# Selective scan with four state numbers by 32 channels on the partitions, and folds of four units every second step

## What is computed

```
xc, r  = split(x @ W_in);  xs = conv4(xc) + conv_b;  u = silu(xs)
dbc    = u @ W_x                                  # 128 columns, then B (16), then C (16)
delta  = softplus(dbc[..., :128] @ W_dt + b_dt)
h[l]   = exp(-delta[l] * A[d, n]) * h[l-1] + delta[l] * u[l] * B[l, n]     # for every d, n
y[l,d] = sum over n of h[l, d, n] * C[l, n]  + u * D
x1     = layernorm(x + (y * silu(r)) @ W_out + xs)
sel    = the 64 rows of x1 with the highest x1 @ w_router, in each batch
out    = x1 with those rows replaced by gate * (attention + MLP)(sel) + (1 - gate) * sel
result = layernorm(x1 + out)
```

## Time and profile before

| | us |
|---|---|
| median of 3 runs | 518.41 |
| lowest and highest | 515.31, 520.69 |
| the profiled execution | 517.08 |
| its span, first to last instruction | 515.3 |

### The profile page before, as it was taken

How to read it: one execution, slowest core, us unless ns; L and a number is a source line. 1 busy time by engine, 2 the same in 40 slices (tenths; PEclk the granted TensorE clock), 3 DMA queues, 4 the chain that set the end, 5 groups by cost and what they waited for, 6 DMA issues and landing times.

```text
span 515.3 us, 6513 instructions
## 1 busy us (share of the span) xinstructions
PE 430.3 (83%) x2021; PEld 256.1 (50%) x2021; DVE 299.1 (58%) x600; ACT 335.4 (65%) x736; POOL 254.3 (49%) x230
## 2 busy tenths in 40 slices
PE   5988988878889869889978689887886888999992
PEld 3433443344435434444534345444484576887881
DVE  0302473368473458856557997869569267553465
ACT  4245697795777696568699649795186298543242
POOL 2010064369456759657467956885554144332012
PEclk9999998989999979999988788979698799999997
DMA  6102400005200001401000413780210000000003
GB/s 223 41 0 83 125 32 31 20 0 128 80 22 26 16 21 31 116 20 37 25 21 2 110 55 103 227 303 23 107 58 1 2 0 1 0 3 1 1 34 129
DMA packets 18710, 29.11 MB, mean 56 GB/s; under 512 B 2698, under 2 KB 10676, under 8 KB 18420
## 3 DMA queue, kind: packets, MB, share of 16 engines
q1 hardware_dynamic: 18676, 28.70, 18.0%
HBM read 22.27 MB, written 2.23 MB: 48 GB/s over the span
## 4 chain that ended last, share of the span: by engine, by line
PE 47%; ACT 23%; DVE 8%; issue 7%; POOL 2%; ACTq 0%; POOLq 0%; DVEq 0%
ACT loop_buf L1022 10%; PE bank L535 9%; PE bank L670 7%; PE bank L551 7%; ACT front_a L1032 5%; PE bank L616 3%; PE bank L846 3%; PE bank L822 3%; PE bank L573 2%; ACT state L1056 2%; DVE state L1184 2%; PE bank L638 1%; PE bank L620 1%; PE bank L854 1%; PE bank L582 1%
## 5 line engine op out<-in xcount | busy, mean ns | idle before, releaser
L1184 DVE TENSOR_TENSOR_SCAN state<-front_a,bank 128x512 f32<-128x512 f32 x88 | 103.9, 1209 | 63.0 <-PE bank L535 37.9
L535 PE MATMUL bank<-ident,loop_buf 128*128 128x128 f32 x512 | 92.7, 302 | 37.4 <-ACT loop_buf L1022 36.9
L535 PEld LDWEIGHTS bank<-ident,loop_buf 128*128 128x128 f32 x512 | 64.4, 151 | 111.3 <-ACT loop_buf L1022 45.8
L1022 ACT ACTIVATE loop_buf<-copy,b_rows 128x256 f32<-128x256 f32 x252 | 105.2, 495 | 0.1
L1032 ACT ACTIVATE front_a<-loop_buf,a_neg 128x512 f32<-128x512 f32 x128 | 84.5, 711 | 6.3 <-DVE state L1184 3.3
L1560 POOL TENSOR_TENSOR state<-state,front_a 128x1024 f32<-128x1024 f32 x22 | 53.7, 2450 | 31.2 <-DVE state L1184 31.0
L1560 POOL TENSOR_TENSOR state<-state,c_own 128x1024 f32<-128x1024 f32 x22 | 51.8, 2358 | 31.0 <-DVE state L1184 31.0
L1184 DVE TENSOR_TENSOR_SCAN copy<-front_a,bank 128x512 f32<-128x512 f32 x40 | 47.6, 1212 | 33.2 <-PE bank L535 20.4
L551 PE MATMUL bank<-front_c,conv_raw 128*128 128x512 f32 x128 | 60.9, 608 | 2.2 <-ACT front_c L897 0.9
L670 PE MATMUL bank<-state,fold 128*64 128x512 f32 x176 | 55.0, 705 | 0.0
L551 PEld LDWEIGHTS bank<-front_c,conv_raw 128*128 128x128 f32 x128 | 23.2, 197 | 23.1 <-issue 21.3
(11 more groups left out here) (202 smaller groups left out, 730.3 us busy)
## 6 DMA issues: line engine op xcount, KB each, us to landing
front_a<-c_stage SPq DMA_DIRECT2D x32, 128.0 KB, 2.9
c_own<-c_stage SPq DMA_DIRECT2D x32, 128.0 KB, 3.0
loop_buf<-front_b SPq DMA_DIRECT2D x32, 128.0 KB, 2.3
copy<-in_L_attn_x SPq DMA_DIRECT2D x4, 512.0 KB, 3.8
front_b<-in_L_ffn_wo SPq DMA_DIRECT2D x1, 2048.0 KB, 10.3
copy<-in_L_ffn_wq SPq DMA_DIRECT2D x1, 2048.0 KB, 8.3
out<-loop_buf SPq DMA_DIRECT2D x3, 512.0 KB, 2.9
conv_raw<-in_L_attn_conv_w SPq DMA_DIRECT2D x2, 512.0 KB, 3.8
```

Source lines behind the costliest of these rows:

```text
L535: return pe.transpose(dst, src, ident[:])
L1022: act.activation(zed[:, g % NZ, c, :, i, :], du_rows[b % 2][:, c, :].rearrange("p (k d) -> p k d", k=2 * KD), ACT.Copy, scale=b_rows[:, b ...
L1184: dve.tensor_tensor_scan(state[t % NH][:, j, :], decay[:, u % NDA, :], bank[BU_BANK[u % NBU]][:], 0.0, ALU.mult, ALU.add).then_inc(scanned, 1)
```

## The change

**Layout.** The partitions of a unit are now four states n by 32 channels. A group is eight units (four steps), and there are four groups a batch. The fold takes four units of two steps at once: `add_states(w)` has four matmuls by a 128x32 matrix, each to its own 32 PSUM partitions and its own 32 columns of the array. It stands in every second step (t odd), and folds steps t-3 and t-2. The number of turns, decays, scans and weighs stays.

**Buffers.** z has two buffers of twice the size. The state slots go from six to four, C from four buffers to two (of four steps each). delta is widened to eight tiles of 512 tokens a batch in a ring of twelve, each with a semaphore of its own (`in_delta[k]`), four DMAs of 32 partitions for a tile: 32 DMAs a batch, sixteen of them (`widen_delta(b, 1)`) after C of the batch's first group. ACT makes the chunks of z of the next group at steps 1 (chunk 0), 2 (chunks 1 and 2) and 3 (chunk 3) of each four, ahead of that step's decays.

**x1** is kept for one batch. It is stored to DRAM after its la pieces (`store_x1`), and all of it is loaded back before the second layer's end (`x1_all`). The softplus pieces s1 to s6 and du stand one step earlier than before.

The core of the diff:

```diff
...
-    -10: ("rs", "cr", "dl0", "dl1"), -9: ("s1",), -8: ("s2",), -7: ("s3",), -6: ("s4",), -5: ("s5", "s6"),
-    -3: ("du0", "du1"),
+    -10: ("rs", "cr", "dl0", "dl1", "s1"), -9: ("s2",), -8: ("s3",), -7: ("s4",), -6: ("s5", "s6"),
+    -4: ("du0", "du1"),
...
-        fold = sb("fold", [P, P // 2])
...
-        NDA, NBU, NH, NZ, NCW = 4, 4, 6, 2, 4
+        fold = sb("fold", [P, QP])
...
+        NDA, NBU, NH, NZ, NCW = 4, 4, 4, 2, 2
+        KB, NDW = 4 * KD, 12
...
-        loop_buf = sb("loop_buf", [P, NZ * 2 * C * DM + 2 * 2 * KD * L])
-        zed = loop_buf[:, 0:NZ * 2 * C * DM].rearrange("p (s c k n d) -> p s c k n d", s=NZ, c=C, k=2 * KD, n=2)
-        delta_wide = loop_buf[:, NZ * 2 * C * DM:].rearrange("p (s i l) -> p s i l", s=2, i=2 * KD)
+        Z_ALL = NZ * 4 * C * DM
+        loop_buf = sb("loop_buf", [P, Z_ALL + KB * L])
+        zed = loop_buf[:, 0:Z_ALL].rearrange("p (s c k n d) -> p s c k n d", s=NZ, c=C, k=KB, n=4)
+        delta_wide = [loop_buf[:, Z_ALL + i * L:Z_ALL + (i + 1) * L] for i in range(KB)]
+        delta_wide += [copies[1][0][:, 4 * KD * L + i * L:4 * KD * L + (i + 1) * L] for i in range(NDW - KB)]
...
-        c_own = sb("c_own", [P, 2 * L])
-        c_wide = [w_inT.rearrange("p k d -> p (k d)"), spare.rearrange("p k d -> p (k d)"), c_own[:, 0:L], c_own[:, L:]]
+        c_wide = [w_inT.rearrange("p k d -> p (k d)"), spare.rearrange("p k d -> p (k d)")]
...
-        in_buf = state_buf[:].rearrange("p (s j l) -> p s j l", s=4, j=2)
-        in_copy = copies[1][0][:, 4 * KD * L:].rearrange("p (s j l) -> p s j l", s=2, j=2)
-        state = [in_buf[:, i] for i in range(4)] + [in_copy[:, i] for i in range(2)]
+        state = state_buf[:].rearrange("p (s j l) -> p s j l", s=NH, j=2)
...
-            def widen_delta(b):
-
-                if b >= 2:
-                    sp.wait_ge(decay_made, 2 * NST * (b - 1))
-                for h in range(KD):
-                    sp.wait_ge(delta_ready, KD * b + h + 1)
-                    for j in range(2):
-                        for i in range(2):
-                            sp.dma_start(delta_wide[i * P // 2:(i + 1) * P // 2, b % 2, 2 * h + j, :],
-                                         delta[j * P // 2:(j + 1) * P // 2, h, :]).then_inc(in_delta[b % 2], 16)
+            def widen_delta(b, h):
+
+                sp.wait_ge(delta_ready, KD * b + h + 1)
+                for j in range(4):
+                    slot = KB * b + 4 * h + j
+                    if slot >= NDW:
+                        b0, k0 = (slot - NDW) // KB, (slot - NDW) % KB
+                        sp.wait_ge(decay_made, 2 * NST * b0 + KB * (NQ - 1) + k0 + 1)
+                    for i in range(4):
+                        sp.dma_start(delta_wide[slot % NDW][i * QP:(i + 1) * QP, :],
+                                     delta[j * QP:(j + 1) * QP, h, :]).then_inc(in_delta[4 * h + j], 16)
+
+            def store_x1(b):
+
+                sp.wait_ge(rows_ready, 2 * (b + 1))
+                sp.dma_start(x1_stage[b], x1[:, :, 0:DM]).then_inc(x1_stored, 16)
...
                 if g >= NCW:
-                    sp.wait_ge(weighed, 2 * (g - NCW + 1))
-                for i in range(2):
-                    sp.dma_start(c_wide[g % NCW][i * P // 2:(i + 1) * P // 2, :],
-                                 c_stage[b, 2 * m + i:2 * m + i + 1, :].partition_broadcast(P // 2)).then_inc(in_c[g % NCW], 16)
+                    sp.wait_ge(weighed, 4 * (g - NCW + 1))
+                for i in range(4):
+                    sp.dma_start(c_wide[g % NCW][i * QP:(i + 1) * QP, :],
+                                 c_stage[b, 4 * m + i:4 * m + i + 1, :].partition_broadcast(QP)).then_inc(in_c[g % NCW], 16)
...
             for g in range(NCW):
                 widen_c(g)
-            widen_delta(0)
+            widen_delta(0, 0)
+            widen_delta(0, 1)
             load_x(2)
-            for g in range(NCW, B * NPAIR - 3):
-                if g % NPAIR == 0:
-                    widen_delta(g // NPAIR)
-                if g == NPAIR:
-                    load_x(3)
+            for g in range(NCW, B * NQ - 2):
+                b, m = g // NQ, g % NQ
                 widen_c(g)
+                if m == 0:
+                    widen_delta(b, 1)
+                elif m == 2 and b >= 1:
+                    store_x1(b - 1)
+                elif m == 3:
+                    if b == 0:
+                        load_x(3)
+                    widen_delta(b + 1, 0)
+            store_x1(B - 2)
 
...
-            sp.wait_ge(in_delta[(B - 1) % 2], 16 * 8 * (B // 2))
+            for k in range(KB):
+                sp.wait_ge(in_delta[k], 64 * B)
...
             load("w_v", w_v, wv.rearrange("(k p) n -> p k n", p=P))
-            widen_c(B * NPAIR - 3)
             load("w_o", w_o, wo.rearrange("(h p) n -> p h n", p=P))
-            widen_c(B * NPAIR - 2)
+            widen_c(B * NQ - 2)
             load("w_dn", w_dn, w_down.rearrange("(f p) n -> p f n", p=P))
-            widen_c(B * NPAIR - 1)
+            widen_c(B * NQ - 1)
...
+            store_x1(B - 1)
+            sp.wait_ge(x1_stored, 16 * B)
+            sp.dma_start(x1_all, x1_stage.rearrange("b p c d -> p b c d")).then_inc(x1_loaded, 16)
...
             def turn_bu(u):
 
-                g, k = u // 4, u % 4
+                g, k = u // KB, u % KB
                 if u >= NBU:
                     pe.wait_ge(scanned, u - NBU + 1)
...
-            def add_states(t):
-
-                b, m, h = t // NST, t % NST // 2, t % 2
+            def add_states(w):
+
+                b, m, h = 2 * w // NST, 2 * w % NST // 4, w % 2
                 if m == 0 and b >= 1:
                     pe.wait_ge(y_taken, KD * (b - 1) + h + 1)
-                pe.wait_ge(weighed, t + 1)
-                for j in range(2):
-                    mm = pe.matmul(bank[Y_BANK[h]][j * P // 2:(j + 1) * P // 2, :], fold[:], state[t % NH][:, j, :],
-                                   start=(m == 0), stop=(m == NPAIR - 1))
+                pe.wait_ge(weighed, 2 * w + 2)
+                for j in range(4):
+                    mm = pe.matmul(bank[Y_BANK[h]][j * QP:(j + 1) * QP, :], fold[:],
+                                   state[:, (2 * w + j // 2) % NH, j % 2, :], start=(m == 0), stop=(m == NQ - 1),
+                                   tile_position=(0, j * QP))
                 mm.then_inc(summed, 1)
...
-                if t >= LAG_ADD:
-                    add_states(t - LAG_ADD)
+                if t % 2 and t >= 3:
+                    add_states((t - 3) // 2)
...
+                    if b >= 1:
+                        wait_filled(act, ("ga", b - 1))
+                        act.wait_ge(chosen_ready, b)
+                        act.wait_ge(x1_stored, 16 * b)
...
-                        ins = act.activation(x1[:, C * b + c, 0:DM], z[:, c, :], ACT.Identity, scale=rstd[:, 0, c:c + 1],
+                        ins = act.activation(x1[:, c, 0:DM], z[:, c, :], ACT.Identity, scale=rstd[:, 0, c:c + 1],
...
-                        act.wait_ge(bu_filled, 4 * (g - NZ + 1))
-                for i in range(2):
-                    n = 2 * m + i
-                    act.activation(zed[:, g % NZ, c, :, i, :], du_rows[b % 2][:, c, :].rearrange("p (k d) -> p k d", k=2 * KD), ACT.Copy,
+                        act.wait_ge(bu_filled, KB * (g - NZ + 1))
+                for i in range(4):
+                    n = 4 * m + i
+                    act.activation(zed[:, g % NZ, c, :, i, :], du_rows[b % 2][:, c, :].rearrange("p (k d) -> p k d", k=KB), ACT.Copy,
                                    scale=b_rows[:, b % 2, c, n:n + 1]).then_inc(z_act, 1)
...
-                if u % (2 * NST) == 0:
-                    act.wait_ge(in_delta[b % 2], 16 * 8 * (b // 2 + 1))
+                b, m, k = u // (2 * NST), u // KB % NQ, u % KB
+                if m == 0:
+                    act.wait_ge(in_delta[k], 64 * (b + 1))
                 if u >= NDA:
                     act.wait_ge(scanned, u - NDA + 1)
-                act.activation(decay[:, u % NDA, :], delta_wide[:, b % 2, k, :], ACT.Exp,
+                act.activation(decay[:, u % NDA, :], delta_wide[(KB * b + k) % NDW], ACT.Exp,
                                scale=a_neg[:, k, m:m + 1]).then_inc(decay_made, 1)
...
             for t in range(B * NST):
-                if t % 2 and t < T_LAST:
-                    make_z(t // 2 + 1, C - 1)
+                if t // 4 + 1 < B * NQ:
+                    for c in ((), (0,), (1, 2), (3,))[t % 4]:
+                        make_z(t // 4 + 1, c)
                 for u in range(2 * t + 2, min(2 * t + 4, NU)):
                     make_decay(u)
-                if t % 2 == 0 and t < T_LAST - 1:
-                    for c in range(C - 1):
-                        make_z(t // 2 + 1, c)
...
                 if t >= NH and j == 0:
-                    dve.wait_ge(summed, t - NH + 1)
-                dve.tensor_tensor_scan(state[t % NH][:, j, :], decay[:, u % NDA, :], bank[BU_BANK[u % NBU]][:], 0.0,
```

(11 more changed lines are left out.)

76 lines of the change are left out of this document (42 added, 34 removed).

## The result

The changed kernel takes 546.12 us (median of 4 runs, 544.34 to 549.39), the kernel before, on the same chip, 517.12. The ratio is 1.056, with an interval of 1.050 to 1.062: 29 us slower, where 6 us faster was forecast, and outside the range. Ratios leave out runs that fell in a slower state of the chip and are not formed from the medians, so the two can differ by up to 3 us. The profiled execution is the slowest of the four (549.39 us); it has a span of 547.7 us and a mean granted clock of 0.852 (before 515.3 and 0.927).

What follows compares the result with a forecast made beforehand. No engine was full; each waited for another in turn, some 84 us a batch. 517.1 - 24 (folds and z handover) + 3 (start) + 2 (four slots) + 13 (last batch) = 511.1 us; range 498 to 526.

Steps and rivals of the forecast that it cites:

- The folds: PE's fold of eight instructions takes 1.05 us for two steps; some 16 us gained before step 56.
- rival D: PE's folds: quarters don't run side by side, a block takes 2.3 us, no gain, 522 us; chance 0.08.
- The handover of z: ACT to PE: waits at one step in four, so PE's wait halves from 36.9 to 18, gaining 18 us.
- Both together, seven tenths: Main loop, 56 steps: folds and z handover could give 34 us; seven tenths, 24 us, is taken.
- rival B: ACT sets the pace and z waits go elsewhere; only the folds pay, 11 us: 524 us; chance 0.15.
- The last batch: +13: Last batch: C of group 14 waits behind x1's store, w_v and w_o; loop ends 13.2 us later.
- Rival A: Last batch: C is not held up behind the weights, costing 5 us and not 13: 503 us; chance 0.17.
- The start: +3: Start of the loop: 32 delta DMAs make decays wait, 3 us lost, between nothing and six.
- Four slots: +2: State slots and shorter lag: PE may wait 1 to 2 us once a batch for a younger weigh.
- rival C: PE's fold at odd t: four slots tie scan, weigh and fold together; 19 us more, 530 us; chance 0.10.
- The shift of the pieces: Softplus one step earlier, put at no cost.

Runs made afterwards that it cites:

- g1: f1 with its fold made in two pairs of 64 columns, half of each weight tile zero, as long as the old fold: 523.93 us, ratio 1.014.
- e3: Changed kernel with z chunks (0,1) and (2,3) in steps 1 and 2 of four, none in the step of the handover: 524.45 us, ratio 1.022.
- f3: Kernel before, with all four chunks of z in the even step, none in the step of the handover: 504.31 us, ratio 0.980.
- f4: Kernel before, with chunks 2 and 3 of z both in the odd step, ahead of its decays: 522.31 us, ratio 1.018.
- e1: Changed kernel with SP's last-batch order changed: C of group 14 ahead of w_o, store of batch 2's x1 last: 534.46 us, ratio 1.042.
- f1: Changed kernel with both edits, the last-batch queue of e1 and the early z of e3: 514.24 us, ratio 0.998.
- g3: f3 with four state slots in place of six: 505.81 us, ratio 0.978.
- g4: Kernel before with only the change's shift of softplus (one step earlier) and du (four steps ahead instead of three): 520.62 us, ratio 1.008.
- f2: f1 with softplus pieces s1 to s6 back at their steps before the change, du still at 4 ahead: 512.75 us, ratio 0.998.
- h3: f1 with z spread evenly: chunk 0 ending step 0, chunks 1 and 2 at step 1, chunk 3 at step 2 ahead of decays: 511.87 us, ratio 0.990.
- g2: Changed kernel with eight turns of the identity ahead of PE's wait for the last chunk of z: 543.86 us, ratio 1.055.

## Why the prediction was wrong

**The folds.** The time of one was right: "1.05 us with four more weight loads" is 1.06 at the full clock, and rival D is out. Eight instructions of 0.43 one by one would be 3.4 us, so the four quarters bring 3.2. The Trainium skill ("TensorE: Matmul & The Clock Gate", on packing small matmuls) gives 3.07 for four row tiles; by it I had 1.12, and the trace is a little better than that. What was too large is "half of it 18, and some 16": 31.6 us of this work are worth 9.7 us (g1).

**The handover of z.** This is the step that failed: "I halve the wait: 36.9 to 18, so 18 us." The wait was 45.2 us, and finishing z in the step of the handover cost 18 us (e3), where the same term cost 10 in the kernel before (f3); so 8 us were lost where 18 were to be gained. I counted handovers and noted that the chunk is twice as long, but multiplied only the number. Number times length, which is how the cost grew from f3 over the kernel before to f4, would have given no gain at all. The second error is in the same paragraph: "the next chunk has two or three steps to spare" supposes an ACT that is ahead of PE. ACT stands in order behind front copies that wait for PE's convolutions, and after such a stop a whole group, 6.6 us of scalings, comes at once with PE waiting at the end of it. With half of the handovers twice the scalings hang on each. How much of the 8 us comes from that stop and how much from the decays between the chunks, no run tells.

**Both together, seven tenths.** The forecast took 24 us from a sum in which both parts had the sign of a gain. Nothing in it stood for the case that a longer chunk costs more per handover; rival B had the waits going elsewhere, and even it gave 524. The batches, which were to take 77 us, take 88 to 90.

**The last batch: +13.** Right in size and in mechanism: C behind the store, w_v and w_o; 12.7 us by the traces, T + 22.8 for scan 60 where T + 23.1 was given. e1 takes most of it out (33.8 us behind T, for 44.5). Rival A is out.

**The start: +3.** At its fifth step f1 is 2.7 us behind f3 (76.45 against 73.72 us for the first scan of step 4, read from DVE's timelines), and the changed kernel 5.8 us behind the kernel before. But at the first scan of batch 1 f1 is only 0.6 us behind f3 (133.6 and 133.0), so there the loss is made up; the changed kernel is still 5.4 behind.

**Four slots: +2.** The ring alone costs nothing that can be measured (g3), and PE waited for the younger weigh only 1.6 us in the changed kernel and 5.5 in f1, where rival C had 19. So C is out in the form it was given. What the ring costs together with folds every second step was not tried. The shift of the pieces, put at nothing, costs 4 us in the kernel before (g4); f2 shows nothing of it for the softplus in the changed one.

**The sum again.** From 517: the queue 8 to 13 and the late end of z 18, together 30 (f1). That is the whole loss against the kernel before, but part of z's 18 us was in that kernel too. Against f3, which has z early in the old layout, f1 is 9 us slower (0.018 of ratio), although its folds give 10. So some 19 us are taken by other things. The start and the shift make at most 5 of them, and no run here settles the rest. h3, some 4 us below f1, may show a part of it to be the bursts of z. By the traces of f1 and f3 it comes late: f1 is behind by 0.6 us at the first scan of batch 1, 1.1 at that of batch 2, 3.6 at that of batch 3, and 6.3 at the end of the loop. Delta copies through SP, folds that come only every second step, and the two C slots in place of four were not tried alone.

## What to carry to other kernels

The cost of handovers goes with the length of the last piece that the waiting engine needs as well as with their number: batching twice the work behind one event halves the number and doubles the piece, which alone gains nothing, and here it cost more. Before counting on fewer waits, look where the last piece stands in its engine's order, and try to finish it a step early; here that one line is worth 2% in the old kernel and 3% in the new. A queue written out by hand must be read again when a transfer is added: what stands ahead of the one transfer that the pace hangs on, and how many bytes.

## What the runs showed of the hardware that was not expected

Eight short turns did not hold the clock up in front of a fold. In the handover of g2 shown above it was 1.00 up to 243.6 us, as the fill began, and 0.51 over the rest of the fill (0.64 over both); over the wait of 0.94 us behind it and over the fold it was 0.50, and the fold took 1.94 us. The windows of g2 over the fill, the wait and the fold:

```profile
243.00:245.20 2.20, 1.88 (x9) 1.48 (x9) 1.42 (x3) 2.20 (x6) 2.01 (x2) 0.64 0.00 0
245.20:246.40 1.20, 0.33 (x1) 0.18 (x1) 1.03 (x1) 1.20 (x4) 1.20 (x2) 0.50 0.00 0
246.40:248.40 2.00, 2.00 (x10) 0.26 (x9) 0.00 (x0) 1.98 (x3) 2.00 (x2) 0.50 0.00 0
```

And less work on PE is partly paid back in its busy time. In the changed kernel the folds are busy for 48.5 us in place of 79.2, 30.7 less, but PE as a whole only 17.3 less (413.0 for 430.3), at a mean clock of 0.852 in place of 0.927; f1 and g1 show the same with nothing else changed (19.6 of 31.6).

A delta copy of 64 KB cost SP 0.63 us to issue, one of 128 KB 0.62, so cutting a transfer in two doubles SP's time for it. An issue of C right behind 3.5 MB cost 1.44 us, and 0.43 where w_o had been issued 15 us before (e1).
